# Spreading 16 bit ids over the partitions by broadcast transfers, and moving the fourth one-hot block to fifth place

## The reference, cut to what matters

```
e = stack([tbl_f[ids[:, f]] for f in range(40)], axis=1)        # (512, 40, 32)
z = einsum('bpd,pde,bpe->bp', e[:, i], W_pair, e[:, j])         # 780 pairs i < j
h = concatenate([z, dense_ctx], axis=1)                          # (512, 796)
h = maximum(h @ W_top1 + b_top1, 0)                              # 512 wide
h = maximum(h @ W_top2 + b_top2, 0)                              # 256 wide
y = h @ W_top3                                                   # (512, 1)
```

## Time and profile before

| | |
|---|---|
| median of 3 runs | 198.24 us |
| the profiled execution | 198.23 us |
| its span | 196.3 us |
| TensorE, DVE, ACT, POOL busy | 182.7, 149.8, 56.3, 106.1 us |
| pair products on DVE (L546) | 100, together 115.6 us |
| one-hot matrices on DVE / on ACT | 27 / 7 |
| first matmul of a one-hot chunk | 10.13 us into the span |
| group 9, the first after block 3 | 50.55 us |
| transpose of block 4 | 56.32 us |

### The profile page before, as it was taken

One profiled execution on the slowest core, in us unless ns is written; L12 is line 12 of the kernel. 1 busy time (PEld: TensorE's weight loads), 2 busy tenths in 40 slices (PEclk: granted clock), 3 DMA queues, 4 the chain that ended last, 5 costly groups with the idle time before them and its releaser, 6 DMA issues.

```text
span 196.3 us, 3798 instructions
## 1 busy us (share of the span) xinstructions
PE 182.7 (93%) x1624; PEld 55.1 (28%) x1624; DVE 149.8 (76%) x148; ACT 56.3 (29%) x58; POOL 106.1 (54%) x114
## 2 busy tenths in 40 slices
PE   3996969599899999999999999999999999998992
PEld 1232313133222322222223222322322322222340
DVE  4869989966798996685699997776969996664502
ACT  4997389993110101112101011201111011112401
POOL 6877777877777777777777777822001002213000
PEclk9999999999999999999999999999999999999999
DMA  5930030300669240051000001000000000000000
GB/s 150 404 133 17 13 94 13 110 12 17 199 179 342 54 147 17 13 159 16 12 13 17 13 13 17 14 0 0 5 0 0 3 0 0 5 0 0 3 0 0
DMA packets 6921, 10.83 MB, mean 55 GB/s; under 512 B 2004, under 2 KB 4440, under 8 KB 6904
## 3 DMA queue, kind: packets, MB, share of 16 engines
q1 hardware_dynamic: 3832, 9.00, 13.7%
q0 software_dynamic: 3072, 1.58, 4.5%
HBM read 10.57 MB, written 0.00 MB: 54 GB/s over the span
## 4 chain that ended last, share of the span: by engine, by line
PE 72%; DVE 1%; ACT 0%; issue 0%; DVEq 0%
PE ps_t L634 27%; PE ps_z L648 24%; PE ps_x L672 10%; PE ps_t L628 4%; PE ps_t L683 4%; PE ps_t L657 2%; PE ps_x L608 2%; DVE prod L556 0%; PE ps_z L692 0%; ACT late_z L477 0%; DVE prod L559 0%; DVEq L555 0%
## 5 line engine op out<-in xcount | busy, mean ns | idle before, releaser
L546 DVE TENSOR_TENSOR prod<-ps_t,xt 128x1024 f32<-128x1024 f32 x100 | 115.6, 1216 | 27.7 <-PE ps_t L634 22.3
L434 POOL DMA_INDIRECT emb<-tbl,idx x96 | 93.8, 978 | 29.6 <-issue 28.9
L634 PE MATMUL ps_t<-xt,w_sb 32*128 32x512 f32 x360 | 58.8, 640 | 0.0
L648 PE MATMUL ps_z<-prod,ones 128*32 128x512 f32 x400 | 53.0, 604 | 0.0
L442 POOL TENSOR_TENSOR late_z<-late_z,tbl_oh 128x512 f32<-128x512 f32 x8 | 10.2, 1277 | 44.6 <-ACT tbl_oh L484 44.6
L634 PEld LDWEIGHTS ps_t<-xt,w_sb 32*128 32x128 f32 x360 | 19.8, 182 | 34.2 <-issue 20.3
L672 PE MATMUL ps_x<-late_z,late_w 128*32 128x512 f32 x192 | 22.8, 592 | 0.0
L503 DVE TENSOR_SCALAR hot_dve<-ids,ramp 128x2048 bf16<-128x2048 f16 x27 | 18.9, 754 | 1.5 <-PE ps_x L596 1.5
L648 PEld LDWEIGHTS ps_z<-prod,ones 128*32 128x32 f32 x400 | 8.1, 108 | 37.9 <-issue 30.3
L484 ACT ACTIVATE tbl_oh<-ps_x 128x512 f32<-128x512 f32 x8 | 4.8, 597 | 40.4 <-PE ps_x L672 40.4
L477 ACT ACTIVATE late_z<-ps_z 128x512 f32<-128x512 f32 x7 | 4.2, 594 | 35.3 <-PE ps_z L648 35.3
(11 more groups left out here) (65 smaller groups left out, 84.5 us busy)
## 6 DMA issues: line engine op xcount, KB each, us to landing
tbl_oh<-small_tables SPq DMA_DIRECT2D x3, 512.0 KB, 4.5
emb<-tbl,idx POOLq DMA_INDIRECT x96, 2.3
late_w<-w SPq DMA_DIRECT2D x1, 1280.0 KB
late_w<-w SPq DMA_DIRECT2D x2, 512.0 KB, 5.0
w_sb<-w_pairs SPq DMA_DIRECT2D x1, 704.0 KB, 4.2
tbl_oh<-small_tables SPq DMA_DIRECT2D x1, 640.0 KB, 6.8
w_sb<-w_pairs SPq DMA_DIRECT2D x1, 640.0 KB, 3.9
w_sb<-w_pairs SPq DMA_DIRECT2D x1, 576.0 KB, 4.1
```

The lines of the kernel that those rows point to most:

```text
L434: nc.gpsimd.indirect_dma_start(emb[:, n % E_RING, t, u * D:(u + 1) * D], None, tables[field], bass.IndirectOffsetOnAxis(ap=idx[:, at:at + ...
L546: nc.vector.tensor_tensor(prod[:, g % PROD_RING, :].rearrange("p (i b) -> p i b", i=2), ps_t[PAIR[g]][:, :].rearrange("p (i b) -> p i b", ...
L634: last = nc.tensor.matmul(o, w_sb[s * D:(s + 1) * D, at:at + P], xt[s * D:(s + 1) * D, kk, :], start=True, stop=True)
L648: last = nc.tensor.matmul(ps_z[q * D:(q + 1) * D, :], ones[:, v * D:(v + 1) * D], prod[:, t // 2 % PROD_RING, t % 2 * B:(t % 2 + 1) * B], ...
```

## The change

The ids of the small fields come from the host's array of input bytes as their lower 16 bits. SP loads each one-hot block's ids by one transfer of its own that reads one row of 2048 int16 (4 KB) and writes it to all 128 partitions (512 KB in SBUF). The 16 spreading matmuls, their selection matrix, the cast and the eight ACT copies are gone. The first table comes in two halves of four chunks with a semaphore and a split for each. The block of the 1250-row tables is now block 4, and block 3 is a looked-up one, transposed after group 6. ACT makes eight matrices instead of seven: two at the start, then 1, 2, 1 and 2 after its copies of blocks 0 to 3. TensorE starts with 11 f32 matmuls of 128 x 128 on `ident` whose result nobody reads. The list becomes

```
-OH_BLOCKS = (0, 1, 2, 3)
+OH_BLOCKS = (0, 1, 2, 4)
...
+TBL_PARTS = [(0, 4), (4, OH_FIRST[1])] + [(OH_FIRST[j], OH_FIRST[j + 1]) for j in range(1, len(OH_BLOCKS))]
+PART_OF_BLOCK = [1 + j for j in range(len(OH_BLOCKS))]
...
-SPLIT_AT = {(0, 4): 1, (1, 4): 2, (2, 3): 3}
-ON_ACT = [(1, 6), (2, 1), (2, 4), (2, 7), (3, 1), (3, 4), (3, 7)]
+SPLIT_AT = {(0, 3): 1, (1, 3): 2, (2, 7): 3}
+WARM_UP = 11
+ON_ACT = [(0, 3), (0, 6), (1, 5), (2, 3), (2, 6), (3, 1), (3, 4), (3, 7)]
+ACT_MAKES_FIRST, ACT_MAKES_AFTER = 2, {0: 1, 1: 2, 2: 1, 3: 2}
...
-XT_AFTER = {3: 5, 4: 5, 5: 7, 6: 9, 7: 11, 8: 13, 9: 15}
+XT_AFTER = {3: 3, 4: 5, 5: 7, 6: 9, 7: 11, 8: 13, 9: 15}
-HOT_BEFORE = {... ("group", 4): [(3, 3)], ("group", 5): [(3, 3)], ("group", 7): [(3, 3)], ("transpose", 3): [(3, 1)]}
+HOT_BEFORE = {... ("group", 7): [(3, 2)], ("group", 9): [(3, 2)], ("group", 10): [(3, 3)], ("group", 12): [(3, 3)]}
...
-        ids_oh = sb("ids16", [P, len(OH_BLOCKS), FB, B], F16)
+        ids_oh = sb("ids16", [P, len(OH_BLOCKS), FB, B], I16)
...  SP
-            sp.dma_start(ids_raw[:, :], ids_oh_rows).then_inc(ids_raw_in, 16)
+            def load_small_ids(j):
+                sp.dma_start(ids_oh[:, j, :, :].rearrange("p f b -> p (f b)"),
+                             ids_oh_rows[j:j + 1, :].broadcast_to([P, FB * B])).then_inc(ids_oh_in[j], 16)
+            load_small_ids(0)
             sp.dma_start(idx[:, :], ids).then_inc(ids_in, 16)
             load_small_tables(0)
             load_small_tables(1)
+            load_small_ids(1)
+            load_small_tables(2)
             load_weights(0)
-            load_small_tables(2)
+            load_small_ids(2)
             load_small_tables(3)
-            for k in range(1, 4):
-                load_weights(k)
+            load_weights(1)
+            load_weights(2)
+            load_weights(3)
+            load_small_ids(3)
+            load_small_tables(4)
             for k in range(4, NK):
                 sp.wait_ge(transposed, k - 2)
                 load_weights(k)
                 if k == MLP_AT:
+                    sp.wait_ge(transposed, OH_BLOCKS[-1] + 1)
...  ACT
-            for h in range(2 * len(OH_BLOCKS)):
-                act.wait_ge(ids_spread, h + 1)
-                nc.scalar.activation(ids_oh[...], ps_t[h % 3][:, :], ACT.Copy).then_inc(ids_oh_made, 1)
...
-            one_hot(0)
+            for _ in range(ACT_MAKES_FIRST):
+                one_hot(act_hots)
+                act_hots += 1
             for what, k in STEPS:
-                if what == "hot" and k in ACT_HOTS and ACT_HOTS.index(k) + 1 < len(ACT_HOTS):
-                    one_hot(ACT_HOTS.index(k) + 1)
                 if what == "transpose":
                     ...
+                    for _ in range(ACT_MAKES_AFTER.get(k, 0)):
+                        one_hot(act_hots)
+                        act_hots += 1
...  DVE
-            nc.vector.tensor_copy(to_all[:, :, :], ...).then_inc(to_all_made, 1)
-            dve.wait_ge(ids_raw_in, 16)
-            nc.vector.tensor_copy(ids_few[:, :], ids_raw[:, :]).then_inc(ids_few_made, 1)
...
-            split_table(0)
-            for n in range(DVE_RING - 1):
-                one_hot(n)
+            one_hot(0)
+            one_hot(1)
+            split_part(0)
+            one_hot(2)
+            split_part(1)
...  TensorE
-            for h in range(2 * len(OH_BLOCKS)):
-                ...
-                for f in range(2):
-                    last = nc.tensor.matmul(ps_t[h % 3][:, f * B:(f + 1) * B], to_all[:, 2 * h + f, :], ids_few[:, :], ...)
-                last.then_inc(ids_spread, 1)
+            pe.wait_ge(ident_made, 1)
+            for _ in range(WARM_UP):
+                nc.tensor.matmul(ps_t[0][:, 0:P], ident[:, :], ident[:, :], start=True, stop=True)
...
+                    if (j, c) == (0, TBL_PARTS[1][0]):
+                        pe.wait_ge(tbl_last_made, 2)
                     if c == 0:
-                        pe.wait_ge(tbl_last_made, j + 1)
+                        pe.wait_ge(tbl_last_made, PART_OF_BLOCK[j] + 1 if j else 1)
...
+def low_halves(ids):
+    return np.ascontiguousarray(np.ascontiguousarray(ids).view(np.int16)[:, ::2])
```

More of the change, by code:

```diff
@@ L28 @@
 I32 = mybir.dt.int32
-F16 = mybir.dt.float16
+I16 = mybir.dt.int16
 BF16 = mybir.dt.bfloat16
@@ L126 @@
 E_RING, PROD_RING, DVE_RING, ACT_RING = 4, 6, 4, 2
-XT_AFTER = {3: 5, 4: 5, 5: 7, 6: 9, 7: 11, 8: 13, 9: 15}
+XT_AFTER = {3: 3, 4: 5, 5: 7, 6: 9, 7: 11, 8: 13, 9: 15}
 HOT_BEFORE = {("transpose", 0): [(0, 8)], ("group", 0): [(1, 2)], ("transpose", 1): [(1, 6)], ("group", 1): [(2, 2)],
-              ("group", 2): [(2, 2)], ("transpose", 2): [(2, 4)], ("group", 4): [(3, 3)], ("group", 5): [(3, 3)],
-              ("group", 7): [(3, 3)], ("transpose", 3): [(3, 1)]}
+              ("group", 2): [(2, 2)], ("transpose", 2): [(2, 4)], ("group", 7): [(3, 2)], ("group", 9): [(3, 2)],
+              ("group", 10): [(3, 3)], ("group", 12): [(3, 3)]}
 EARLY = [((0, 1), (26, 30, 34, 40)), ((2, 3), (56, 62, 68, 76)), ((4, 5), (88, 92, 96, 99))]
@@ L340, in dlrm_tower @@
         neg_ramp_made = sem("neg_ramp_made")
-        ids_raw_in, ids_few_made, to_all_made = sem("ids_raw_in"), sem("ids_few_made"), sem("to_all_made")
-        ids_spread, ids_oh_made = sem("ids_spread"), sem("ids_oh_made")
-        tbl_in = [sem(f"tbl_in{j}") for j in range(len(OH_BLOCKS))]
+        ids_oh_in = [sem(f"ids_oh_in{j}") for j in range(len(OH_BLOCKS))]
+        tbl_in = [sem(f"tbl_in{n}") for n in range(len(TBL_PARTS))]
         tbl_rest_made, tbl_last_made = sem("tbl_rest_made"), sem("tbl_last_made")
@@ L451, in one_hot @@
                 j, c = ACT_HOTS[n]
+                if n == 0 or ACT_HOTS[n - 1][0] != j:
+                    act.wait_ge(ids_oh_in[j], 16)
                 wait_slot(act, ACT_HOTS, n, ACT_RING, hot_used_act)
@@ L504, in one_hot, with split_part @@
                                         ramp[:, at:at + 1], None, ALU.is_equal).then_inc(hot_made_dve, 1)
[L506 to L509 removed]
+            def split_part(n):
+                cols = part_cols(n)
+                dve.wait_ge(tbl_in[n], 16)
                 nc.vector.tensor_tensor(tbl_rest[:, cols], tbl_oh[:, cols], upper_halves(tbl_oh[:, cols]),
                                         ALU.subtract).then_inc(tbl_rest_made, 1)
[L512 removed]
+                dve.wait_ge(tbl_rest_made, n + 1)
                 nc.vector.tensor_tensor(tbl_last[:, cols], tbl_rest[:, cols], upper_halves(tbl_rest[:, cols]),
                                         ALU.subtract).then_inc(tbl_last_made, 1)
[L516 to L520 removed]
             nc.vector.memset(ones[:, :], 0.0).then_inc(ones_zero, 1)
@@ L536, in _ @@
                     if k in SPLIT_AT:
[L537 removed]
+                        split_part(PART_OF_BLOCK[SPLIT_AT[k]])
                 elif what == "group":
@@ L562, in _ @@
         def _(pe):
-            pe.wait_ge(to_all_made, 1)
-            pe.wait_ge(ids_few_made, 1)
-            for h in range(2 * len(OH_BLOCKS)):
-                if h >= 3:
-                    pe.wait_ge(ids_oh_made, h - 2)
-                for f in range(2):
-                    last = nc.tensor.matmul(ps_t[h % 3][:, f * B:(f + 1) * B], to_all[:, 2 * h + f, :], ids_few[:, :],
-                                            start=True, stop=True)
-                last.then_inc(ids_spread, 1)
+            pe.wait_ge(ident_made, 1)
+            for _ in range(WARM_UP):
+                nc.tensor.matmul(ps_t[0][:, 0:P], ident[:, :], ident[:, :], start=True, stop=True)
             for what, k in STEPS:
@@ L616, in _ @@
                         pe.wait_ge(moved, OH_BLOCKS[2] + 1)
-                    else:
-                        pe.wait_ge(ids_oh_made, 2 * len(OH_BLOCKS))
                     kk, _, i = TILES[2 * g]
@@ L748 @@
         "ids": np.ascontiguousarray(a["ids"].reshape(BT, P, F).transpose(1, 0, 2)).reshape(P, BT * F),
-        "ids_oh": np.ascontiguousarray(a["ids"].T[OH_FIELDS]).reshape(len(OH_BLOCKS), FB * B),
+        "ids_oh": low_halves(a["ids"].T[OH_FIELDS]).reshape(len(OH_BLOCKS), FB * B),
         "small_tables": laid_out_small_tables([a[f"tbl_{f}"] for f in OH_FIELDS]),
```

28 lines of the change are left out of this document (8 added, 20 removed).

## The result

The changed kernel takes 193.27 us (median of four, 193.11 to 193.5) against 198.31 (198.16 to 199.68) for the kernel before on the same chip: a ratio of 0.968 (95% interval 0.9631 to 0.9729). The profiled execution took 193.5, its span 191.7. The forecast was 192.6. On the chips of the experiments the kernel before ran at 198.2 to 198.8 us where its mean granted clock was 1.00 and up to 200.8 where it was 0.991, so its medians there are 200.17, 200.06 and 199.80; the changed kernel gave 192.9 to 193.5 on the two chips that it ran on. Because of that I compare the experiments by the start of group 14 in the profiled executions first, and by medians second. Each of these starts comes from one execution: the two of the changed kernel differ by 0.14 us, and those with the old ids by 0.8 to 1.0 us already at group 0, where their lists are still the same.

A forecast was written before the change was run, and what follows sets the result against it. TensorE, busy 93% of the span, was taken as the bound, though before 50 us no engine works all the time; gains of 3.1 and 2.5, together 5.6, took 198.23 to 192.6 us, range 190.6 to 196.6.

The forecast's parts named there:

- Group 14 sets the end: From group 14 the step list is unchanged, so the remaining 139.4 us move as a block.
- Ids landed at 4.5: Block 0's ids, SP's first transfer, land 3.8 us after issue at 0.74, so at 4.5.
- neither the half nor the quarter of the rate: Rival, slow broadcast of the ids: 196.4 us at a quarter of 411 GB/s, 193.9 at half; chance 0.16.
- The start up to table 1: DVE's matrices and splits from the first ids at 4.5 to the end of table 1's split at 14.4.
- Block 0 at 13.7, group 0 at 16.5, group 1 at 25.2, block 2 at 31.3: TensorE's early schedule: blocks 0 and 2 complete, groups 0 and 1 start at these times; 3.1 us gained by block 2.
- a sign of being wrong: TensorE waiting more than half a microsecond for ACT's matrices would show the forecast wrong.
- Block 3 looked up, 2.5: Block 2 to group 14: block 3 looked up, one-hot chunks between groups, 2.5 us gained, no gather waits.
- The sum as 3.1 + 2.5: Gain at group 14: 3.1 us from blocks 0 to 2 plus 2.5 from block 3's new order, 5.6.
- DVE becomes the tight engine: From first matrix to product 13, DVE, not TensorE, is tight; its 45.2 us of work caps the gain at 7.9.
- ACT: hidden: ACT loses 7.44 us of copies and gains one matrix pair; taken as hidden, no effect on the time.
- The warm-up at nothing, the half tables at no gain: Before block 0: 11 first matmuls over before 7.7 cost nothing, 0.3 us for half-pace chunks unbooked; no gain for table halves.
- The int16 comparison: Rival: DVE's 26 matrices slow from int16, 203.4 us at 1.23 each, 231 at 2.3; chance 0.08.

The follow-up runs named there:

- own rows: The changed kernel with the host's int16 ids laid out 128 times, so each partition reads its own row: 192.53 us, ratio 0.9625.
- the variant with the old ids and the new ACT rule: The kernel before with the changed kernel's block order and its rule that ACT makes matrices after its block copies: 196.98 us, ratio 0.9871.
- the variant with the old order: The changed kernel with one-hot blocks 0, 1, 2, 3 and the step order from before the change: 198.71 us, ratio 0.9957.
- the memsets: The changed kernel with a 128 x 512 memset ahead of each of DVE's 26 one-hot matrices: profiled execution 203.09 us, only other run 257.63.
- the old ids and the old rule: The kernel before with the changed kernel's block order; ACT makes its next matrix when the list reaches a chunk of ACT's: 201.79 us, ratio 1.0089.
- gaps filled: The changed kernel with group 0 behind block 1, burst 0 before group 4, block 3's transposes before burst 1: 199.46 us, ratio 0.9981.

## Why the prediction was right, and where it was not

The measured median of 193.27 is 0.7 above the forecast of 192.6 and inside 190.6 to 196.6. By its steps:

- **Group 14 sets the end.** Right: 139.8 us from there to the end of the span, 139.4 before.
- **Ids landed at 4.5.** Measured 5.2. The own rows show why: the broadcast costs 1.1 us in landing, of which 0.6 arrive at group 14. My price of 3.8 from issue, taken from other loads, lies between the 4.45 of the broadcast and the 3.3 of own rows. The Trainium skill's rule ("DMA: Bandwidth & Descriptors", section "Latency and other measured facts") on slow loads is about rows 512 KiB or more apart in HBM; here rows 4 KiB apart load faster than one row read 128 times, so the case is outside it, and neither the half nor the quarter of the rate that I priced came.
- **The start up to table 1.** I had DVE end table 1's split at 14.4, and it ends at 14.44 though DVE started 0.8 later. Half splits at 1.34 instead of 1.5, matrices at 0.66 to 0.68, and no wait of 0.2 for the half table gave back what the ids took. Two errors cancelled, and that is luck: the landing was too early and the prices of DVE too high.
- **Block 0 at 13.7, group 0 at 16.5, group 1 at 25.2, block 2 at 31.3.** Measured 14.59, 16.75, 25.18, 31.68. Block 0 is 0.9 late, most of it because ACT's matrix (0,6) starts out from the later ids and is there at 13.1 instead of 12.35; block 1 waits for DVE anyway, and group 1 is on time. TensorE's wait of 0.68 for that matrix is over the half microsecond that I had named as a sign of being wrong; my own schedule had 0.75 there (7.7 + 6 x 0.65 to 12.35), so the sign was badly chosen. Between group 1 and block 2 I missed 0.4: groups 2 and 3's matmuls and four chunks take 1.18 + 2.86 = 4.0 instead of 3.8, and they start 0.1 later. This and 0.3 behind block 2 are what is missing at group 14 (51.87 against 51.2).
- **Block 3 looked up, 2.5.** From block 2's completion to group 14 it is 51.87 - 31.68 = 20.2 us against 56.90 - 34.4 = 22.5 before: 2.3. The transposes came at 36.56, the gathers had landed, and no gather wait is in the trace. The variant with the old ids and the new ACT rule needs the same 20.2, so this term stands by itself.
- **The sum as 3.1 + 2.5.** Measured 2.7 and 2.3. The second term is there without the first. The first is there at block 2 without the second, but does not last: in the variant with the old order DVE has the last block's table split, two products and that block's first matrix due right behind block 2, and 0.3 is left at group 14. Whether another share of matrices would have kept it with the old order, no run shows. DVE starts at 5.3 here and at 5.5 before; what the change does is to fill its waits.
- **DVE becomes the tight engine.** Right up to 23.6, by the chain. Behind that the chain is TensorE's, with copies of ACT's, and the memsets show that DVE had 3.5 us to give in the whole stretch. Product 13 came 4.3 earlier, against the bound of 7.9 from DVE alone.
- **ACT: hidden.** Wrong as a reason. It is hidden only since ACT makes its matrices behind the copies. With the old ids and the old rule the same order costs 4.5 us more at group 14 and is 0.9% slower than the kernel before. My schedule followed the changed kernel's rule, but no term of the sum says that it depends on it.
- **The warm-up at nothing, the half tables at no gain.** Too low: 0.85 and about 2 us at the median, 0.5 and 0.4 at group 14.
- **The int16 comparison.** 0.68 each. The rival with the largest price was empty; the Trainium skill's rule ("VectorE: DVE Perf Modes", section "What auto-detection actually checks") that element size and layout decide agrees with this trace.
- **Late loads, the second layer's weights, four more SP entries.** At nothing, as priced.

What I don't know is where the runs of the kernel before at 200 us, and those of the one with the table in one piece above 195.3, lose their time against the profiled executions. The mean granted clock of the former is 0.991 instead of 1.00; a fall like the ones above would fit, but none of these runs has a trace.

## What to carry to other kernels

Before adding up the gains of two edits, write down for each engine the earliest time at which its own queue can be done, with one edit and with both: where a different engine binds in each case, an early gain of one edit (2.7 us here) can be lost again (to 0.3) before it reaches the end. Before calling a part's gain small, compare the stretches that it doesn't touch: here 0.8 us of a difference lay ahead of the part under test. When a step is moved, follow what each other engine has chained to it, and put the copy that frees a buffer ahead of any work that only has to be done some time. Don't let TensorE stand for long ahead of dense work: behind the stops of 2.65 us and more in these traces part of the stop was paid a second time in the clock.

## What the runs showed of the hardware

**The clock falls in the middle of a kernel.** I had looked only at the start. TensorE's stops and the granted clock behind them: 1.93 us (the changed kernel at 23.76), 1.00; 2.65 us (new ids, old order), 0.58 and 0.57 in 34 to 38; 2.73 us (memsets, at 30.49), 0.50 in 32 to 34; 3.17 us (table in one piece), 0.55 in 8 to 10; 3.38 us (old ids, new order), a group at 1.94 instead of 1.09; 5.64 us (gaps filled), 0.50 in 44 to 46; 5.93 us (ids behind the table), 0.50 until about 16. Behind each of these stops of 2.65 us and more, equal matmuls ran at the 1.2 GHz level at first, so time was lost a second time.

**The record of the clock doesn't tell all.** In the kernel without the warm-up and in the repetition of the changed one, equal groups of four matmuls step by 0.43 and later by 0.21, with the granted clock at 1.00 in both stretches, as in the earlier trace rows. The pace of equal matmuls tells the level where the record doesn't. The Trainium skill ("TensorE: Matmul & The Clock Gate", section "What you observe") has the doubling vary by half a microsecond from run to run; here two executions of one kernel differ by more, full pace by 8.21 and by 10.95, and so do two with the old ids whose matmuls are the same up to there, 12.66 and 14.7.

**A broadcast read has a price.** 512 KB as one 4 KB row read 128 times landed 1.1 us later than as 128 rows, and in 2.5 to 3.5 us, with both still on their way, the DMA moved 281 instead of 347 GB/s.
